# An embedding tower on one Trainium2 core: an eleventh table by matmul, a gather ring of 2 KB, and whole layer parts between the gram pieces

## The chip, the core and the metric

One core of a Trainium2 chip runs the whole kernel. The metric is the device time of one execution in microseconds. Three runs of the kernel before took 398.37, 398.69 and 398.92 us; the median is 398.69.

## What is computed

2048 samples have 128 dense features and one id in each of 26 tables with rows of 128 floats. One table has 125000 rows, eight have 12500, ten 1250 and seven 1000. The reference, cut to what matters:

```python
e = jnp.stack([tbl_0[ids[:, 0]], ..., tbl_25[ids[:, 25]]], axis=1)      # 2048 x 26 x 128
combined = jnp.concatenate([dense[:, None, :], e], axis=1)              # 2048 x 27 x 128
gram = jnp.einsum('bfd,bgd->bfg', combined, combined)                   # 27 x 27 a sample
z = jnp.concatenate([dense, gram[:, TRIU_I, TRIU_J]], axis=1)           # 128 + 351
h = jnp.concatenate([z, dense], axis=1)                                 # 607
h = jnp.maximum(h @ W_top1 + b_top1, 0.0)                               # 607 -> 512
h = jnp.maximum(h @ W_top2 + b_top2, 0.0)                               # 512 -> 256
y = h @ W_top3                                                          # 256 -> 1
```

Everything is float32.

## The kernel before, in words

The samples are cut into 16 tiles of 128, taken as 8 pairs (`i`): an even and an odd tile. Each engine has its own program, written out by hand, and they meet at semaphores. A table reaches the features in one of two ways.

**By gather** (16 tables, `GATHERED`). POOL issues one indirect DMA per tile and table (L328), 32 a pair, into `emb`, which has three tile slots. PE transposes four tables at a time into a PSUM bank (`flip`, L346) and ACT copies the bank into `feats` (`keep_flipped`, L544). A gather waits until the slot's old content is flipped, and for `pace` (L244): a place in PE's program, from the list of weighted steps in `places_of` (L212).

**By matmul** (the 10 smallest tables, `LOOKED_UP`; they stay in SBUF as an exact sum of two parts, `hi` and `lo`). A table is held in chunks of 125 rows: 8 chunks for 1000 rows, 10 for 1250. For each chunk DVE compares the ids of a pair's 256 samples with the row numbers and writes a matrix of zeros and ones (`mark`, L568, the operation at L580, "a mark"); PE multiplies `hi` and `lo` of the chunk by it (`look_up`, L350, L364). That is 7 x 8 + 3 x 10 = 86 marks and 172 matmuls a pair. `marks` is a ring of `MARK_CHUNKS` = 28 chunks. So DVE makes at most `AHEAD` = 7 halves of a table (28 marks) ahead of a pair's lookups. Two tables share a bank of the three in `flip_ps`, and ACT copies them out (`keep_looked`, L618, L622).

**The turn of a pair** on PE: all lookups of pair `i` (with `pair_rows` of the odd tile before among them), then `even_gram(i)` (L447), then `odd_gram(i)` (L474). The gram of a tile is 8 pieces (`gram`, L372, L386) of 16 float32 products of 27 x 27. Between the pieces stand the `flip`s of the next tile (4 a tile) and the layers of the pair before: `layer(i - 1, 0..3)` are the 512 outputs of the first layer, four products each; `layer(i - 1, 4)` and `5` the 256 of the second, four each; then `third_layer`. A part of a layer is split over several gaps with the argument `parts`. Of layer 3 the first two products stand before the even tile's last piece, the other two behind it. A float32 product of these layers and of the gram is recorded as two matmuls.

DVE, in order: `lay_out` (L549) of the even tile, which transposes the gram's result (L558) and copies the pairs out (L566), as soon as the even tile's last gram piece is done; 28 marks for the next pair; `lay_out` of the odd tile; the other 58 marks. For pairs 0 to 2 the flips of the even tile stand among the lookups instead of in the odd gram (`EARLY`).

**Start-up.** SP loads the ten tables into room that later holds something else (`places`, L124: five in `feats`, then `dots`, `w2_sb`, `hT`, `w1p_sb`; the tenth again in `dots`, when `lo` of the sixth is done, L291). ACT rounds each to `hi` (L674), DVE makes `lo` (L588) and the marks of pair 0. ACT's program has the lookups' copies among the roundings: the third copy and those of tile 0's flips stand behind the tenth rounding. The ids of the next pair (`id_cols`, 640 KB) are loaded when all marks of a pair are made (L302).

The four lines that say what waits in start-up:

```python
if s >= PLACES:
    sp.wait_ge(s_lo, place(s) + 1)          # SP, L291
act.wait_ge(s_raw[place(s)], ...)           # ACT, L673
dve.wait_ge(s_looked, g - MARKS_BACK[h] + 1)  # DVE, L578
```

## Time and profile before

| | |
|---|---|
| median of three runs | 398.69 us (398.37 to 398.92) |
| the profiled execution's own time | 400.2 us |
| its span in the profile | 398.3 us |
| PE busy / DVE / ACT / POOL | 364.5 / 261.1 / 137.0 / 247.2 us |
| marks (DVE L580) | 688, 211.5 us |
| lookup matmuls (PE L364) | 1376 |
| gathers (POOL L328) | 256, 247.0 us |
| mean granted TensorE clock | 0.983 of full speed |

The span is what the profile covers; the sums below are made against it. PE is the matmul engine (its weight loads are a row of their own, PEld), DVE the vector engine, ACT the scalar engine, POOL issues gathers and SP the plain DMAs. Matmul records overlap: what one costs is read from start to start. A busy share is an average over the start-up (to about 68 us), the seven turns and the tail (from about 372 us), which have different limits.

### The profile page before, as it was taken

The numbers are of one execution on the slowest core, as the hardware profiler recorded it, in microseconds if no ns is written. First come the engines' busy times: TensorE is split into PE (matmuls) and PEld (weight loads), VectorE is DVE, ScalarE is ACT, GpSimd is POOL, SyncE is SP. The second block draws the span as 40 slices with busy tenths as digits, with TensorE's granted clock in tenths as the row PEclk, the third lists the DMA queues.
The fourth block names the chain that finished last, engine by engine and source line by source line (L and its number), as shares of the span: only waits on it lengthen the run. The fifth ranks groups of instructions, "written<-read, shape, count | busy, mean of one in ns | idle before, by whom it ended". The sixth has DMA issues, their size and how long they took to land.

```text
span 398.3 us, 13947 instructions
## 1 busy us (share of the span) xinstructions
PE 364.5 (92%) x6192; PEld 309.7 (78%) x6192; DVE 261.1 (66%) x748; ACT 137.0 (34%) x195; POOL 247.2 (62%) x260
## 2 busy tenths in 40 slices
PE   0857758999999999999999999999999999999798
PEld 0757747987689977997789876997789877997575
DVE  2999864990699409990599519990699419980310
ACT  3545130343325234323433334323433334324222
POOL 6777777777677665776677666775677666720000
PEclk9998996999999999999999999999999999999989
DMA  7953442223112311323122311313121312200000
GB/s 242 411 195 110 149 144 57 54 55 120 49 42 55 113 43 44 82 53 115 43 55 55 114 49 44 81 54 109 48 51 53 116 47 51 54 22 2 5 2 0
DMA packets 13677, 31.72 MB, mean 80 GB/s; under 512 B 5301, under 2 KB 6205, under 8 KB 13618
## 3 DMA queue, kind: packets, MB, share of 16 engines
q0 software_dynamic: 8192, 16.79, 15.9%
q1 hardware_dynamic: 5426, 14.04, 9.7%
q8 instruction: 49, 0.80, 0.9%
q14 instruction: 10, 0.08, 0.1%
HBM read 30.81 MB, written 0.01 MB: 77 GB/s over the span
## 4 chain that ended last, share of the span: by engine, by line
PE 48%; DVE 44%; issue 4%; DMA 3%; ACT 1%; SPq 0%
DVE marks L580 37%; PE flip_ps L364 12%; PE mlp_ps L412 11%; PE gram_ps L386 9%; PE flip_ps L346 6%; PE mlp_ps L421 5%; PE mlp_ps L415 3%; DVE dots L558 3%; DVE lo L588 3%; DMA feats<-small_rows 1%; DMA id_cols<-ids_in_pairs 1%; DVE pair_dots L566 1%; PE mlp_ps L430 1%; PE pairs_ps L397 1%; ACT feats L622 0%
## 5 line engine op out<-in xcount | busy, mean ns | idle before, releaser
L328 POOL DMA_INDIRECT emb<-tbl,idx x256 | 247.0, 965 | 103.8 <-issue 55.8
L580 DVE TENSOR_SCALAR marks<-id_cols,row_no 125x256 fp32r<-125x256 int16 x688 | 211.5, 384 | 4.9 <-DMA id_cols<-ids_in_pairs 4.9
L364 PE MATMUL flip_ps<-marks,hi 125*128 125x256 f32 x688 | 172.2, 291 | 18.4 <-DVE marks L580 18.0
L364 PE MATMUL flip_ps<-marks,lo 125*128 125x256 f32 x688 | 167.9, 284 | 0.0
L364 PEld LDWEIGHTS flip_ps<-marks,hi 125*128 125x128 f32 x688 | 132.6, 193 | 26.0 <-issue 21.3
L364 PEld LDWEIGHTS flip_ps<-marks,lo 125*128 125x128 f32 x688 | 132.7, 193 | 0.0
L558 DVE STREAM_TRANSPOSE dots<-gram_ps 128x864 f32<-128x864 f32 (+1 forms) x32 | 25.2, 824 | 105.8 <-PE gram_ps L386 105.8
L622 ACT COPY feats<-flip_ps 128x512 f32<-128x512 f32 x40 | 46.7, 1167 | 124.4 <-PE flip_ps L364 119.4
L386 PEld LDWEIGHTS gram_ps<-feats 128*27 128x27 f32 x4096 | 43.0, 106 | 44.4 <-issue 43.3
L544 ACT COPY feats<-flip_ps 128x512 f32<-128x512 f32 x64 | 45.0, 725 | 64.9 <-PE flip_ps L346 62.8
L386 PE MATMUL gram_ps<-feats 128*27 128x27 f32 x4096 | 54.9, 192 | 10.2 <-issue 6.8
L412 PE MATMUL mlp_ps<-xT,w1p_sb 117*128 117x256 f32 x192 | 53.6, 391 | 0.5 <-ACT y_sb L657 0.5
L346 PE MATMUL flip_ps<-ident,emb 128*128 128x128 f32 x256 | 41.0, 285 | 2.7 <-ACT feats L622 2.3
L421 PE MATMUL mlp_ps<-hT,w_sb 128*128 128x256 f32 x128 | 36.6, 404 | 0.0
L412 PEld LDWEIGHTS mlp_ps<-xT,w1p_sb 117*128 117x128 f32 x192 | 32.5, 190 | 4.2 <-ACT xT L642 1.0
L649 ACT ACTIVATE hT<-mlp_ps,b_sb 128x256 f32<-128x256 f32 x48 | 22.7, 474 | 36.4 <-PE mlp_ps L415 23.2
L346 PEld LDWEIGHTS flip_ps<-ident,emb 128*128 128x128 f32 x256 | 27.0, 141 | 5.8 <-ACT feats L622 3.0
L421 PEld LDWEIGHTS mlp_ps<-hT,w_sb 128*128 128x128 f32 x128 | 23.0, 199 | 2.9 <-issue 0.3
L415 PE MATMUL mlp_ps<-dense_sb,w1d_sb 128*128 128x256 f32 x64 | 19.8, 391 | 0.0
L642 ACT COPY xT<-pairs_ps 117x384 f32<-117x384 f32 x16 | 8.4, 522 | 16.5 <-PE pairs_ps L397 16.5
L566 DVE COPY pair_dots<-dots 128x351 f32<-128x351 f32 x16 | 12.6, 788 | 0.5
L415 PEld LDWEIGHTS mlp_ps<-dense_sb,w1d_sb 128*128 128x128 f32 x64 | 11.1, 190 | 1.2
(23 smaller groups left out, 63.6 us busy)
## 6 DMA issues: line engine op xcount, KB each, us to landing
id_cols<-ids_in_pairs SPq DMA_DIRECT2D x7, 640.0 KB
emb<-tbl,idx POOLq DMA_INDIRECT x256, 2.5
feats<-small_rows SPq DMA_DIRECT2D x5, 512.0 KB, 7.5
dense_sb<-dense_columns SPq DMA_DIRECT2D x4, 256.0 KB, 9.2
w1p_sb<-w_pairs SPq DMA_DIRECT2D x1, 702.0 KB
hT<-small_rows SPq DMA_DIRECT2D x1, 640.0 KB, 12.6
w1p_sb<-small_rows SPq DMA_DIRECT2D x1, 640.0 KB, 14.5
dots<-small_rows SPq DMA_DIRECT2D x1, 640.0 KB, 4.0
```

The costliest lines, as they stand in the source:

```text
L328: nc.gpsimd.indirect_dma_start(emb[:, v, (f - 1) * P:f * P], None, tables[order[f - 1]][:, :], bass.IndirectOffsetOnAxis(ap=idx[:, t, orde ...
L346: last = nc.tensor.transpose(flip_ps[:, m % FLIP_BANKS, (f - 1) % GROUP, :], emb[:, v, (f - 1) * P:f * P], ident[:, :])
L364: last = nc.tensor.matmul(flip_ps[:, m % FLIP_BANKS, 2 * (s % 2):2 * (s % 2) + 2, :], part[s][0:R[s], half * x + c, :], marks[0:R[s], MARK ...
L386: last = nc.tensor.matmul(gram_ps[QUAD * j:QUAD * j + F, n, 0:F], row, row, start=True, stop=True)
L412: last = nc.tensor.matmul(bank, w1p_sb[0:CHUNK, c, q * P:(q + 1) * P], xT[0:CHUNK, c, :, :], start=(c == 0), stop=False)
L415: last = nc.tensor.matmul(bank, w1d_sb[:, q * P:(q + 1) * P], dense_sb[:, i % DENSE_PAIRS, :], start=False, stop=True)
L421: last = nc.tensor.matmul(bank, w2_sb[:, c, (q - H1C) * P:(q - H1C + 1) * P], h1T[:, c, :], start=(c == 0), stop=(c == H1C - 1))
L544: copy(feats[:, u, :, 1 + GROUP * k:1 + GROUP * k + n], flip_ps[:, m % FLIP_BANKS, 0:n, :].rearrange("d f p -> d p f")).then_inc(s_kept[u], 1)
L558: nc.vector.transpose(dots[:, g0 * QUAD:(g0 + n) * QUAD].rearrange("p (g f) -> p g f", f=QUAD), gram_ps[:, :, 0:n].rearrange("p n g -> p g ...
L580: last = nc.vector.tensor_scalar(marks[0:R[s], MARKS_AT[h] + c, :], id_cols[0:R[s], s, :], row_no[0:R[s], s, half * x + c:half * x + c + 1 ...
L622: nc.scalar.copy(feats[:, :, :, f:f + n].rearrange("d u p f -> d f u p"), flip_ps[:, m % FLIP_BANKS, 0:2 * n, :].rearrange("d (f u) p -> d ...
L649: nc.scalar.activation(h[:, c, :], mlp_ps[:, q % 2, 0:2 * P], ACT.Relu, bias=b[:, c:c + 1]).then_inc(s_act, 1)
```

## The change

Three things are changed. An eleventh table, of 1250 rows, is looked up by matmul, so 15 tables are gathered, in groups of 4, 4, 4 and 3. The room for it comes from the descriptor ring of the gathers, which had 16 KB a partition and now has 2 KB. And the layers stand in whole parts between gram pieces. The order in `places_of` and on ACT follows. The ring of marks stays at 28 chunks. Table eleven is loaded into `hT`, when `lo` of the eighth table is done (`place(10)` is 7).

```diff
-LOOKED_UP = 10
+LOOKED_UP = 11
...
-            places += [piece(even, 0)] + flips(odd, 0) + [piece(even, 1), piece(even, 2)] + flips(odd, 1)
-            places += part_of_layers(1) + [piece(even, 3), piece(even, 4)] + flips(odd, 2) + [piece(even, 5)]
-            places += part_of_layers(2) + [piece(even, 6)] + flips(odd, 3) + [piece(even, 7)] + part_of_layers(3)
...
+            for k in range(GROUPS):
+                places += [piece(even, 2 * k)] + flips(odd, k) + [piece(even, 2 * k + 1)] + part_of_layers(k + 1)
...
-                gram(2 * i, 0)
-                flip(2 * i + 1, 0)
-                layer(i - 1, 1, range(0, 1))
-                gram(2 * i, 1)
-                layer(i - 1, 1, range(1, 3))
-                gram(2 * i, 2)
...
-                layer(i - 1, 3, range(1, 2))
-                gram(2 * i, 7)
-                layer(i - 1, 3, range(2, 4))
+                for k in range(GROUPS):
+                    gram(2 * i, 2 * k)
+                    flip(2 * i + 1, k)
+                    gram(2 * i, 2 * k + 1)
+                    if k + 1 < H1C:
+                        layer(i - 1, k + 1)
...
-                layer(i - 1, 4, range(0, 2))
+                layer(i - 1, H1C)
                 gram(2 * i + 1, 0)
                 next_flip(0)
-                layer(i - 1, 4, range(2, 3))
                 gram(2 * i + 1, 1)
+                next_flip(1)
+                gram(2 * i + 1, 2)
                 pair_rows(2 * i)
-                layer(i - 1, 4, range(3, 4))
-                gram(2 * i + 1, 2)
-                next_flip(1)
-                layer(i - 1, 5, range(0, 1))
                 gram(2 * i + 1, 3)
-                layer(i - 1, 5, range(1, 3))
+                layer(i - 1, H1C + 1)
                 gram(2 * i + 1, 4)
                 next_flip(2)
-                layer(i - 1, 5, range(3, 4))
                 gram(2 * i + 1, 5)
-                third_layer(i - 1, range(0, 1))
+                next_flip(3)
                 gram(2 * i + 1, 6)
-                next_flip(3)
+                third_layer(i - 1)
                 gram(2 * i + 1, 7)
-                third_layer(i - 1, range(1, 2))
...
+            layer(last - 1, H1C)
             for part in range(PIECES):
                 gram(tiles - 1, part)
                 if part == 3:
                     pair_rows(tiles - 2)
-            layer(last - 1, 4)
-            layer(last - 1, 5)
+            layer(last - 1, H1C + 1)
             pair_rows(tiles - 1)
             third_layer(last - 1)
...
-    nc = bacc.Bacc("TRN2", target_bir_lowering=False, num_devices=1)
+    nc = bacc.Bacc("TRN2", target_bir_lowering=False, num_devices=1, dynamic_dma_scratch_size=2048)
```

PE, the end of the even tile's gram in a turn in the middle, before. A row is a run of like instructions; L412 and L415 are products of the first layer, L421 of the second, L386 a gram piece, L346 a flip:

```order
L346 MATMUL flip_ps<-ident,emb 128x128 x4
L412 MATMUL mlp_ps<-xT,w1p_sb 128x256
L386 MATMUL gram_ps<-feats 27x27 x16
L415 MATMUL mlp_ps<-dense_sb,w1d_sb 128x256
L412 MATMUL mlp_ps<-xT,w1p_sb 128x256
L386 MATMUL gram_ps<-feats 27x27 x16
L346 MATMUL flip_ps<-ident,emb 128x128 x4
L412 MATMUL mlp_ps<-xT,w1p_sb 128x256
L386 MATMUL gram_ps<-feats 27x27 x16
L412 MATMUL mlp_ps<-xT,w1p_sb 128x256
L415 MATMUL mlp_ps<-dense_sb,w1d_sb 128x256
L421 MATMUL mlp_ps<-hT,w_sb 128x256 x2
```

And of the change (its line numbers are one to two lower there):

```order
L345 MATMUL flip_ps<-ident,emb 128x128 x4
L385 MATMUL gram_ps<-feats 27x27 x16
L411 MATMUL mlp_ps<-xT,w1p_sb 128x256 x3
L413 MATMUL mlp_ps<-dense_sb,w1d_sb 128x256
L385 MATMUL gram_ps<-feats 27x27 x16
L345 MATMUL flip_ps<-ident,emb 128x128 x3
L385 MATMUL gram_ps<-feats 27x27 x16
L420 MATMUL mlp_ps<-hT,w_sb 128x256 x4
```

The last two products of layer 3 stood behind the even tile's last gram piece; now all four stand before its last two pieces, and behind the last piece comes layer 4 as a whole. The flip before the last piece has three tables in place of four.

ACT in start-up, before (L674 rounds a table, L622 copies a bank of lookups, L544 a flipped bank):

```order
L622 COPY feats<-flip_ps 128x2x256
L674 CAST hi<-dots 125x1280
L622 COPY feats<-flip_ps 128x2x256
L633 COPY feats<-dense_sb 128x256
L544 COPY feats<-flip_ps 128x128x4 x4
L622 COPY feats<-flip_ps 128x2x256 x2
```

And of the change:

```order
L599 COPY feats<-flip_ps 128x2x256
L651 CAST hi<-dots 125x1280
L651 CAST hi<-hT 125x1280
L599 COPY feats<-flip_ps 128x2x256
L610 COPY feats<-dense_sb 128x256
L521 COPY feats<-flip_ps 128x128x4 x3
L521 COPY feats<-flip_ps 128x128x3
L599 COPY feats<-flip_ps 128x2x256 x2
L599 COPY feats<-flip_ps 128x256
```

The eleventh rounding stands between the tenth and the third copy of lookups, and so ahead of the copies of tile 0's flips.

## Rows read from the trace of the kernel before

**Rows 1.** The page, chain that ended last: shares of the span by line

```profile
DVE marks L580 37%; PE flip_ps L364 12%; PE mlp_ps L412 11%; PE gram_ps L386 9%; PE flip_ps L346 6%; PE mlp_ps L421 5%; PE mlp_ps L415 3%; DVE dots L558 3%; DVE lo L588 3%; DMA feats<-small_rows 1%; DMA id_cols<-ids_in_pairs 1%; DVE pair_dots L566 1%; PE mlp_ps L430 1%; PE pairs_ps L397 1%; ACT feats L622 0%
```

**Rows 2.** Windows of one turn: length, then PE, PEld, DVE, ACT, POOL busy

```profile
225.67:237.22 11.55, 11.55 (x270) 8.33 (x268) 0.00 (x0) 4.87 (x8) 6.74 (x8) 1.00 0.30 101
237.22:248.73 11.51, 11.51 (x333) 8.29 (x332) 10.86 (x32) 4.88 (x9) 7.61 (x8) 1.00 0.18 48
248.73:270.17 21.44, 21.17 (x177) 20.90 (x177) 20.05 (x61) 6.06 (x8) 16.17 (x17) 1.00 0.27 71
```

**Rows 3.** Timeline of DVE, one turn: start, us, engine, line, operation, count

```profile
237.84 1.58 DVE L558 STREAM_TRANSPOSE dots<-gram_ps 128x864 f32<-128x864 f32 x2 [13.50 <-PE gram_ps L386]
...
240.16 8.45 DVE L580 TENSOR_SCALAR marks<-id_cols,row_no 125x256 fp32r<-125x256 int16 x28
248.53 1.56 DVE L558 STREAM_TRANSPOSE dots<-gram_ps 128x864 f32<-128x864 f32 x2
...
250.84 17.98 DVE L580 TENSOR_SCALAR marks<-id_cols,row_no 125x256 fp32r<-125x256 int16 x58
```

**Rows 4.** The chain in order of time: start us, us, what

```profile
268.87 1.46 PE flip_ps L364 x10
270.33 1.30 PE mlp_ps L412 x6
...
337.87 7.72 PE flip_ps L364 x64
```

**Rows 5.** Timeline of PE in the gram phase of the same turn

```profile
227.50 0.42 PE L386 MATMUL gram_ps<-feats 128*27 128x27 f32 x32
227.85 0.66 PE L346 MATMUL flip_ps<-ident,emb 128*128 128x128 f32 x4
228.34 0.60 PE L412 MATMUL mlp_ps<-xT,w1p_sb 117*128 117x256 f32 x2
228.87 0.42 PE L386 MATMUL gram_ps<-feats 128*27 128x27 f32 x32
229.22 1.13 PE L412 MATMUL mlp_ps<-xT,w1p_sb 117*128 117x256 f32 x4
230.28 0.42 PE L386 MATMUL gram_ps<-feats 128*27 128x27 f32 x32
```

**Rows 6.** Timeline of DVE in the last turn, where gathers end on the way

```profile
339.92 17.03 DVE L580 TENSOR_SCALAR marks<-id_cols,row_no 125x256 fp32r<-125x256 int16 x58
```

**Rows 7.** The gathers as a group (busy, mean ns, idle), and their landing

```profile
L328 POOL DMA_INDIRECT emb<-tbl,idx x256 | 247.0, 965 | 103.8 <-issue 55.8 <-PE gram_ps L386 20.5 <-PE flip_ps L364 12.9
...
emb<-tbl,idx POOLq DMA_INDIRECT x256, 2.5
```

**Rows 8.** Start-up, timelines of SP, then ACT, then DVE: start us, us

```profile
28.23 0.33 SPq L259 DMA_DIRECT2D dots<-small_rows  x1
...
32.22 1.26 ACT L674 CAST hi<-dots 125x1280 fp32r<-125x1280 f32 x1 [3.38 <-DMA dots<-small_rows]
...
34.43 1.53 DVE L588 TENSOR_TENSOR lo<-hT,hi 125x1280 fp32r<-125x1280 f32 x1
...
44.62 3.05 DVE L580 TENSOR_SCALAR marks<-id_cols,row_no 125x256 fp32r<-125x256 int16 x10
...
53.19 5.03 DVE L580 TENSOR_SCALAR marks<-id_cols,row_no 125x256 fp32r<-125x256 int16 x16 [4.93 <-DMA id_cols<-ids_in_pairs]
```

**Rows 9.** Start-up, timeline of PE: the first lookups after the flips

```profile
36.15 0.38 PE L364 MATMUL flip_ps<-marks,hi 125*128 125x256 f32 x1
...
38.81 0.41 PE L364 MATMUL flip_ps<-marks,lo 125*128 125x256 f32 x1
39.02 0.41 PE L364 MATMUL flip_ps<-marks,hi 125*128 125x256 f32 x1
```

**Rows 10.** The tail, timeline of PE, then DVE

```profile
377.37 5.41 PE L421 MATMUL mlp_ps<-hT,w_sb 128*128 128x256 f32 x16
...
379.13 0.77 DVE L566 COPY pair_dots<-dots 128x351 f32<-128x351 f32 x1
```

More of the change, by code:

```diff
@@ L82, in tower @@
     AHEAD = max(h for h in range(1, HALVES + 1) if sum(SIZES[:h]) <= MARK_CHUNKS)
-    assert CHUNKS == 3 and H1C == 4 and H2C == 2 and GROUPS == 4
+    assert H1C == GROUPS == 4 and H2C == 2 and PIECES == 2 * GROUPS
     ctx = ExitStack()
@@ L399, in pair_rows, with layer @@
                 last.then_inc(s_pairs, 1)
-            def layer(i, q, parts=range(4)):
+            def layer(i, q):
                 bank = mlp_ps[:, q % 2, 0:2 * P]
-                if q == 0 and 0 in parts:
+                if q == 0:
                     pe.wait_ge(s_xT, 2 * i + 2)
-                if q != 1 and (i or q) and 0 in parts:
+                if q != 1 and (i or q):
                     pe.wait_ge(s_act, STEPS * i + max(q - 1, 0))
-                for c in parts:
-                    if q < H1C and c < CHUNKS:
-                        last = nc.tensor.matmul(bank, w1p_sb[0:CHUNK, c, q * P:(q + 1) * P],
-                                                xT[0:CHUNK, c, :, :], start=(c == 0), stop=False)
-                    elif q < H1C:
-                        last = nc.tensor.matmul(bank, w1d_sb[:, q * P:(q + 1) * P],
-                                                dense_sb[:, i % DENSE_PAIRS, :], start=False, stop=True)
-                    else:
+                if q < H1C:
+                    for c in range(CHUNKS):
+                        nc.tensor.matmul(bank, w1p_sb[0:CHUNK, c, q * P:(q + 1) * P],
+                                         xT[0:CHUNK, c, :, :], start=(c == 0), stop=False)
+                    last = nc.tensor.matmul(bank, w1d_sb[:, q * P:(q + 1) * P],
+                                            dense_sb[:, i % DENSE_PAIRS, :], start=False, stop=True)
+                else:
+                    for c in range(H1C):
                         if q == H1C:
@@ L422, in layer, with third_layer @@
                                                 h1T[:, c, :], start=(c == 0), stop=(c == H1C - 1))
-                if 3 in parts:
-                    last.then_inc(s_mm, 1)
-            def third_layer(i, parts=range(H2C)):
-                for c in parts:
+                last.then_inc(s_mm, 1)
+            def third_layer(i):
+                for c in range(H2C):
                     pe.wait_ge(s_act, STEPS * i + H1C + c + 1)
@@ L431, in third_layer @@
                                             start=(c == 0), stop=(c == H2C - 1))
-                if H2C - 1 in parts:
-                    last.then_inc(s_mm, 1)
+                last.then_inc(s_mm, 1)
             def looking_up(i, groups=range(LOOK_GROUPS)):
@@ L451, in even_gram @@
                 layer(i - 1, 0)
-                gram(2 * i, 0)
-                flip(2 * i + 1, 0)
-                layer(i - 1, 1, range(0, 1))
-                gram(2 * i, 1)
-                layer(i - 1, 1, range(1, 3))
-                gram(2 * i, 2)
-                flip(2 * i + 1, 1)
-                layer(i - 1, 1, range(3, 4))
-                gram(2 * i, 3)
-                layer(i - 1, 2, range(0, 2))
-                gram(2 * i, 4)
-                flip(2 * i + 1, 2)
-                layer(i - 1, 2, range(2, 3))
-                gram(2 * i, 5)
-                layer(i - 1, 2, range(3, 4))
-                layer(i - 1, 3, range(0, 1))
-                gram(2 * i, 6)
-                flip(2 * i + 1, 3)
-                layer(i - 1, 3, range(1, 2))
-                gram(2 * i, 7)
-                layer(i - 1, 3, range(2, 4))
+                for k in range(GROUPS):
[4 more added lines that the diff above has]
+                        layer(i - 1, k + 1)
             def odd_gram(i):
```

28 lines of the change are left out of this document (11 added, 17 removed).

## The prediction

> **What bounds the kernel now.** I read the page's chain first. Its largest line is DVE's marks, 37% of the span, ahead of every line of PE [rows 1], although PE is busy 364.5 us and DVE 261.1. A kernel bound by PE all the time would not show that, so I cut one turn of the middle into three windows at PE's milestones [rows 2]: the even tile's gram with layers 0 to 3 (11.55 us, DVE idle all of it), the odd tile's gram (11.51 us, DVE busy 10.86), the lookups (21.44 us, DVE busy 20.05). The turn is 44.5 us. DVE's timeline shows why [rows 3]: it waits 13.50 us for the even tile's last gram piece, starts at 237.84, and from there has no pause to speak of. `lay_out`, 28 marks (8.45 us), the second `lay_out`, 58 marks (17.98 us) end at 268.82. PE then does the last half table and layer 0 starts at 270.33 [rows 4]. The loop that sets the turn is thus: DVE from even gram to last mark, 31.0 us; PE's last half table, 1.5; PE's even half of the gram up to DVE's next start, 12.0. The sum is 44.5. The odd half of the gram is not in it: it runs under DVE's first `lay_out` and 28 marks, and ends just as these do.
>
> What PE alone would need is close behind. At full clock 64 lookup matmuls take 7.72 us, 0.12 each [rows 4], so 86 chunks take 20.7 us and with `pair_rows` 21.1; the window has 21.44. PE has 0.3 us a turn to spare, no more.
>
> POOL is not on the path. A gather is 0.965 us [rows 7] and one starts every 1.25 us at the closest; 32 take 40.0 us of the turn's 44.5. Among the waits there is none of PE for a gather, while POOL waits 20.5 us for gram pieces alone, to keep its pace [rows 7].
>
> **The price of a mark.** Two stretches of 58 marks differ: 17.98 us with 14 gathers beside them [rows 3], 17.03 us in the last turn with 9, where the gathers end [rows 6]. The difference of 0.95 us over 5 gathers is 0.19 us a gather, which leaves (17.98 - 14 x 0.19)/58 = 0.264 us a mark. The eleventh table removes gathers and adds marks, and a window of 68 marks will hold about 14 gathers still, since POOL's pace follows PE: 68 x 0.264 + 14 x 0.19 = 20.6 us, 2.6 more than now. The bounds are 2.6 and, at 0.31 us a mark throughout, 3.1.
> The Trainium skill (SBUF — State Buffer, Who interferes with whom) says that a vector instruction with one SBUF input, outside the two-port modes, does not contend with GpSimd at all. If the marks are such, the gathers are not why the two stretches differ, a mark is 0.31 us whatever POOL does, and the sum below would be 3.5 us higher. The rows look otherwise, and I go by them.
>
> **The change, part by part.**
> - *Ten more marks a pair.* They come after `AHEAD` = 28, in the stretch that is on the loop: +2.6 us in each of turns 1 and 3 to 6. In the last turn PE, not DVE, ended the lookups, by 0.3 us, so +2.3 there. In turn 2 PE is slower than DVE (its flips of tile 4 stand among the lookups): PE has 20 matmuls more, 20 x 0.12 = 2.4 us, and its odd half is 0.9 us shorter (a point below), which leaves +1.4; DVE's own path comes out the same there.
> - *Twenty more matmuls a pair*, 2.4 us, beside the marks: hidden, since DVE is slower per chunk. If DVE's marks cost nothing more, they would be what is late next.
> - *Layer 3 whole in the even half.* Two float32 products move from behind the even tile's last piece to ahead of it. A product is two recorded matmuls, six of which take 1.30 us [rows 4]: 0.43 us each. The even half is on the loop, so +0.87 us a turn. The flip of three tables in place of four gives back 0.10. Net +0.77 us, seven times.
> - *Whole parts.* Do they save by fewer switches? Behind a gram piece two products take 1.06 us where 0.87 is their work; one product between a flip and a gram piece takes 0.53 us, where 0.43 is work [rows 5]. So going from and to gram pieces costs 0.10 us each. But the change leaves something between every two gram pieces, seven gaps in the even half before and after. No switch goes. I cost the regrouping at nothing, with bounds of -0.3 and +0.3 us a turn.
> - *The odd half* loses 0.87 + 0.10, gets back some 0.3 since `third_layer` is no longer spread, and ends near 10.8 us after the last even piece, where DVE's `lay_out` may start only when its 28 marks are made, at 11.3. It is hidden, with PE's slack now about 1.3 us a turn. If the odd half were stretched by more than that, it would count.
> - *DVE's transposes before the odd gram*: they end 2.2 us after the last even piece starts. Before, 2.0 us of layer work stood there; now layer 4 (4 x 0.43 + 0.20 = 1.93 us), and the odd gram starts at 2.28. Cover still just holds.
> - *Two gathers a pair fewer*, 16 x 1.25 us of POOL: nothing, as no one waits for POOL. Through a ring of 2 KB they cost what they do now, I take: a gather lands in 2.5 us [rows 7] and starts every 1.25, so two or three are under way at once. The trace shows no full ring; the price is bounded below by 0 and above by a gather that waits for the one before it, 0.965 + 2.5 us.
> - *Start-up.* Table eleven goes to `hT`, whose load may begin when DVE's eighth `lo` is done, at 35.9. The tenth was issued at 28.23 and was ready for ACT at 32.22, 4.0 us [rows 8]; so the eleventh is at 39.9. ACT's third copy of lookups and tile 0's flips stand behind that rounding, and PE's fourth group of lookups behind them. That group began 3.9 us after the last rounding did (36.15 against 32.22, [rows 8, 9]), so now at 43.8. PE is idle meanwhile, and restarts at the lower clock: 0.213 us a matmul (38.81 to 39.02, [rows 9]). The seventh table's 16 matmuls end at 47.3. DVE has by then filled the ring of 28 chunks and stands before the tenth table's marks, which it began at 44.62 [rows 8]. From 47.3: five marks and the wait for the next half (to about 50.4), `lo` 1.4, ten marks 3.0, to 54.8. Before, the last mark ended at 47.6. The start-up is 7.3 us longer (4.4 of it would be the table's own marks and `lo`, the rest is the wait). The ids of pair 1 are loaded after that and all follows: DVE waited 4.93 us for them [rows 8], and will again. Bounds: 6.0 with PE at full clock, 8.3 with a longer slow stretch.
> - *The tail.* Layer 4 of pair 6 moves from behind the last gram to ahead of it, where PE waited for DVE's transposes. Behind the gram, layers 4 and 5 took 5.41 us together [rows 10], at less than full clock; one of them leaves, 2.7 us; `pair_rows` can't start before DVE's copy is through at 379.90 [rows 10], against 382.6 now, so at most 2.7 is gained. I take -2.4; bounds -2.7 and 0.
>
> Sum: start-up 7.3; turn 1 2.6 + 0.4 (there POOL runs unpaced, so two more gathers fall beside the marks) + 0.8 = 3.8; turn 2 1.4 + 0.8 = 2.2; turns 3 to 6 4 x 3.4 = 13.6; turn 7 2.3 + 0.8 = 3.1; tail -2.4. Together **+27.6 us**. The span of 398.3 becomes 425.9, the profiled execution's 400.2 becomes 427.8, and the median 398.69 becomes 426.3.
>
> **The rivals.**
> - *PE becomes the bound.* If the marks come cheaper than I think (fewer gathers beside them), PE alone has: even half 12.3, odd half 10.8, lookups 192 x 0.12 + 0.4 = 23.5, together 46.6 us, 2.1 over now. Then turns 3 to 6 give 8.4 and turn 7 2.6: 7.3 + 3.8 + 2.2 + 8.4 + 2.6 - 2.4 = 21.9, so 420.6 us. For it: PE's slack is only 1.3 us a turn. Against it: ten marks would have to cost under 1.3 us, and the lowest price in the rows is 0.264 each.
> - *The ring is too small.* If a gather must wait for room until an earlier one has landed, up to 3.5 us each, POOL becomes the bound from 47.8/30 = 1.6 us a gather. At 1.9 us, 240 gathers take 456 us, and with the 47 us that follow the last gather now the kernel takes some 503 us. Against it: two or three gathers in flight are few. Nothing in the trace shows a ring's limit.
> - *Faster, because the gathers were the bound.* If POOL's train of 256 x 1.25 us = 320 us set the time and the rest hung on it, 16 gathers fewer would give -20 us: 378.7 us. It would decide if PE stood waiting for gathers. Against it: POOL is the one that waits, by its pace [rows 7], and PE and DVE have no time for the extra work.
>
> **The numbers.** My forecast has 0.76, PE as the bound 0.16, the ring 0.05, the faster case 0.01; 0.02 is left for an effect much smaller than any of these (half each to no change and to faster). The range takes in PE as the bound, with a start-up 1.3 cheaper and 0.3 us a turn gained by the whole parts (417), and upward the marks at 0.31 us (+3.5), no gain in the tail (+2.4) and a start-up 1 us longer: 433. The ring's case is left out. A measurement can tell 0.2% (0.8 us) from no change. Faster by more than that has 0.02, within it 0.01, slower 0.97.
>
> **What would show it.** Right: turns of about 47.9 us in the middle; DVE's stretch of 68 marks near 20.6 us, directly before the last half table of each turn; DVE's idle time before the even `lay_out` about 14.3 us; PE stalls of 1 to 2 us in the lookups for marks; ACT's eleventh rounding near 40, PE idle from 32 to 42, the last mark of pair 0 near 55. Wrong: turns of 46 us with PE never waiting; gathers longer than 1 us or PE waiting for them; an even half of the gram shorter than 12 us (then whole parts do save something); stalls in the odd half that reach DVE's second `lay_out`.

## The result, and the profile after

| | kernel before | the change |
|---|---|---|
| median of 4 runs each | 398.81 us (398.37 to 399.10) | 426.87 us (426.37 to 428.43) |
| ratio, 95% interval | | 1.0711 (1.0681 to 1.0741) |
| profiled execution: time, span | 400.2, 398.3 us | 426.6, 424.8 us |
| mean granted clock of TensorE | 0.983 | 0.976 |
| PE busy, DVE busy | 364.5, 261.1 us | 381.5, 278.6 us |

The change is 7% slower. The forecast was 426.3 us with a range of 417 to 433, slower with 0.97. The median is met within 0.6 us (the span, 424.8 against 425.9, within 1.1), but that is partly luck: the start-up was off by 3.5 us and the turns together by 3.8, in opposite directions. A table shows it best. Each stretch ends at the start of a `lay_out` on DVE, of tile 1 or of the next even tile, and its length is compared before and after.

| stretch | forecast | measured (spans) |
|---|---|---|
| start-up, up to tile 1's `lay_out` | +7.3 | +10.8 (65.67 to 76.45) |
| turn 1 | +3.8 | +2.7 |
| turn 2 | +2.2 | +2.3 |
| turns 3 to 6 | 4 x 3.4 | 2.8, 2.8, 2.7, 2.9 |
| turn 7 | +3.1 | +2.7 |
| tail, behind the last even `lay_out` | -2.4 | -3.15 (27.65 to 24.50) |
| sum | +27.6 | +26.5 |

One plain word on the experiments: three of their four series fell on chips, called slow below, on which the kernel before had a median of 500 to 505 us (the series with `order_alone_b` and `grouped` had it at 398.43 us), so of these only distances inside a trace and ratios are used, and each ratio is of the fast runs alone while the medians are of all runs.

**The chain.** The page of the change, shares of the span by engine and line, to be held against [rows 1]:

```profile
PE 64%; DVE 27%; issue 4%; DMA 2%; ACT 1%; SPq 0%
PE flip_ps L363 24%; DVE marks L557 23%; PE mlp_ps L411 11%; PE gram_ps L385 10%; PE flip_ps L345 8%; PE mlp_ps L420 6%; PE mlp_ps L413 3%; DVE lo L565 2%; DMA feats<-small_rows 1%; DVE dots L535 1%; PE mlp_ps L428 1%; PE pairs_ps L396 1%; DMA hT<-small_rows 1%; DVE pair_dots L543 1%; ACT hi L651 1%
```

The marks had 37% before and have 23% now, though there are more of them; PE's lookups had 12% and have 24%. The shares overstate the move. In turns 2, 3, 4 and 6 the chain leaves DVE 11 marks before the last one and follows PE's last 30 lookup matmuls, and in turns 5 and 7 it stays on PE through all lookups; but in each of turns 4, 5 and 7 the last mark ends 1.32 us before the lookups do, which is PE's last half table. DVE and PE end each of these turns almost together.

**One turn.** Windows of a turn in the middle, cut as [rows 2] are: length, then PE, PEld, DVE, ACT, POOL busy:

```profile
199.01:211.30 12.29, 12.29 (x274) 9.43 (x272) 0.00 (x0) 4.66 (x8) 7.60 (x9) 1.00 0.31 102
211.30:222.00 10.70, 10.70 (x328) 8.17 (x328) 9.88 (x32) 4.89 (x9) 7.58 (x4) 1.00 0.12 28
222.00:246.38 24.38, 24.02 (x196) 23.18 (x196) 23.02 (x71) 6.79 (x8) 17.97 (x18) 1.00 0.21 51
```

The even half grew from 11.55 to 12.29 us, the odd half shrank from 11.51 to 10.70, the lookups grew from 21.44 to 24.38. The cut at 222.00 lies 0.21 us behind PE's first lookup, at 221.79; cut there, as [rows 2] is, the odd half is 10.50 us and the lookups are 24.59. The turn is 47.4 us, forecast 47.9. PE is busy 47.0 of it.

DVE's timeline over the same turn answers to [rows 3]; the last two rows are of the next turn:

```profile
211.82 1.58 DVE L535 STREAM_TRANSPOSE dots<-gram_ps 128x864 f32<-128x864 f32 x2 [14.13 <-PE gram_ps L385]
...
214.12 7.57 DVE L557 TENSOR_SCALAR marks<-id_cols,row_no 125x256 fp32r<-125x256 int16 x28
221.96 1.58 DVE L535 STREAM_TRANSPOSE dots<-gram_ps 128x864 f32<-128x864 f32 x2 [0.27 <-PE gram_ps L385]
...
224.29 20.77 DVE L557 TENSOR_SCALAR marks<-id_cols,row_no 125x256 fp32r<-125x256 int16 x68
...
261.49 7.91 DVE L557 TENSOR_SCALAR marks<-id_cols,row_no 125x256 fp32r<-125x256 int16 x28
...
272.16 20.11 DVE L557 TENSOR_SCALAR marks<-id_cols,row_no 125x256 fp32r<-125x256 int16 x68
```

Three numbers are as forecast: 68 marks in 20.77 us (20.6), DVE idle 14.13 us ahead of the even `lay_out` (14.3), and the even half above (12.3). Two are not. The 28 marks ahead take 7.57 us where [rows 3] had 8.45, and DVE then waits 0.27 us for the odd gram. So the first part of the loop is no longer DVE's `lay_out` and 28 marks but PE's odd half: from one `lay_out` to the other it is 10.14 us (211.82 to 221.96), where [rows 3] has 10.69. In the next turn, turn 5, the 28 take 7.91 and the 68 take 20.11. With the same cuts, the odd half, the lookups and the even half are

| turn | odd half | lookups | even half | together | the 68 marks |
|---|---|---|---|---|---|
| 4 | 10.50 | 24.59 | 12.29 | 47.4 | 20.77 |
| 5 | 10.99 | 23.93 | 12.29 | 47.2 | 20.11 |
| 7 | 10.49 | 23.70 | 12.30 | 46.5 | 19.86 |

The lookups are as long as the marks make them. Turn 5's odd half holds a stall of PE (0.26 us of idle time before 264.24, with nothing to wait for) that the others have not.

**A gather that hangs.** The cheaper 28 marks have a visible companion. POOL's timeline around the same stretch of an earlier turn (DVE makes its 28 marks from 166.74 to 174.31 there):

```profile
167.48 0.94 POOL L327 DMA_INDIRECT emb<-tbl,idx  x1 [0.74 <-PE flip_ps L345]
169.70 4.73 POOL L327 DMA_INDIRECT emb<-tbl,idx  x1 [1.27 <-PE gram_ps L385]
```

One gather lasts 4.73 us and ends at 174.43, 0.12 us after the marks. It happens so in four of the turns, 4.73 to 4.76 us each. In turn 1 it is worse: 80 marks run from 78.75 to 100.79, and one gather hangs for most of that, to 94.73. It doesn't last to the end of the marks, but there is a break in them where it ends: DVE does nothing from 94.60 to 94.70, the only such break among the 80.

```profile
79.59 15.14 POOL L327 DMA_INDIRECT emb<-tbl,idx  x1 [1.96 <-PE flip_ps L363]
```

The group's mean went from 965 ns [rows 7] to

```profile
L327 POOL DMA_INDIRECT emb<-tbl,idx x240 | 265.5, 1106 | 113.0 <-issue 47.9
```

Nobody waits for such a gather. While it hangs, POOL issues no others, and the marks beside it run at their price alone: 28 x 0.264 = 7.4 us.

**Start-up.** DVE in the change, to be held against [rows 8]:

```profile
44.16 1.48 DVE L565 TENSOR_TENSOR lo<-dots,hi 125x1280 fp32r<-125x1280 f32 x1
48.80 3.00 DVE L557 TENSOR_SCALAR marks<-id_cols,row_no 125x256 fp32r<-125x256 int16 x10 [3.16 <-PE flip_ps L363]
51.72 1.48 DVE L565 TENSOR_TENSOR lo<-hT,hi 125x1280 fp32r<-125x1280 f32 x1
53.12 3.04 DVE L557 TENSOR_SCALAR marks<-id_cols,row_no 125x256 fp32r<-125x256 int16 x10
...
61.64 5.03 DVE L557 TENSOR_SCALAR marks<-id_cols,row_no 125x256 fp32r<-125x256 int16 x16 [4.88 <-DMA id_cols<-ids_in_pairs]
67.21 1.58 DVE L535 STREAM_TRANSPOSE dots<-gram_ps 128x864 f32<-128x864 f32 x2 [0.54 <-PE gram_ps L385]
...
76.45 1.58 DVE L535 STREAM_TRANSPOSE dots<-gram_ps 128x864 f32<-128x864 f32 x2 [6.82 <-PE gram_ps L385]
```

and what it waited for, the eleventh table's load on SP, its rounding on ACT, and PE's restart:

```profile
36.94 0.33 SPq L258 DMA_DIRECT2D hT<-small_rows  x1
```

```profile
41.06 1.26 ACT L651 CAST hi<-hT 125x1280 fp32r<-125x1280 f32 x1 [6.56 <-DMA hT<-small_rows]
42.22 1.09 ACT L599 COPY feats<-flip_ps 128x512 f32<-128x512 f32 x1
```

```profile
43.37 1.93 PE L345 MATMUL flip_ps<-ident,emb 128*128 128x128 f32 x7 [9.55 <-ACT feats L599]
44.98 0.58 PE L363 MATMUL flip_ps<-marks,hi 125*128 125x256 f32 x1
45.35 0.42 PE L363 MATMUL flip_ps<-marks,lo 125*128 125x256 f32 x1
```

The load takes 4.1 us as forecast (36.94 to 41.06), PE stands 9.55 us and restarts at 0.21 us a matmul; the granted clock is 0.50 from 43.37 to 48.50, the lower of its two levels (1.2 against 2.4 GHz). The last mark of pair 0 ends at 56.1, 8.5 us later than before; 54.8 was forecast. What the forecast did not have comes behind it. PE's gram of tiles 0 and 1:

```profile
61.09 0.41 PE L385 MATMUL gram_ps<-feats 128*27 128x27 f32 x31
63.22 0.42 PE L385 MATMUL gram_ps<-feats 128*27 128x27 f32 x33 [1.72 <-issue]
...
68.94 1.34 PE L385 MATMUL gram_ps<-feats 128*27 128x27 f32 x118 [1.79 <-DVE dots L535]
72.33 2.06 PE L385 MATMUL gram_ps<-feats 128*27 128x27 f32 x128 [2.05 <-issue]
76.06 0.34 PE L385 MATMUL gram_ps<-feats 128*27 128x27 f32 x10 [1.67 <-issue]
```

"Issue" is time in which PE waited for nothing that the profile shows. Tile 1's gram has two such stalls, 2.05 and 1.67 us; before it had one of 1.81. Tile 0's has stalls of 1.72 (shown) and 1.22 us, and 0.76 ahead of it; before there were 1.41 within it and 1.22 ahead of it, and DVE did not wait for them. Together they turn +8.45 at DVE's 16 marks (61.64 against 53.19) into +9.1 at tile 0's `lay_out` and +10.8 at tile 1's.

**The tail.** PE, the answer to [rows 10]:

```profile
403.82 0.29 PE L385 MATMUL gram_ps<-feats 128*27 128x27 f32 x10
405.33 1.23 PE L385 MATMUL gram_ps<-feats 128*27 128x27 f32 x118 [1.22 <-issue]
406.49 1.99 PE L420 MATMUL mlp_ps<-hT,w_sb 128*128 128x256 f32 x8
409.06 0.59 PE L396 MATMUL pairs_ps<-ident,pair_dots 128*117 128x128 f32 x3 [0.57 <-DVE pair_dots L543]
```

One layer (8 matmuls, 1.99 us, at full clock) and a wait of 0.57 stand where 5.41 us of two layers stood: 2.57 us to `pair_rows` in place of 5.24. The other half microsecond is the smaller stall, 1.22.

### The profile page after: what moved, and what is told of

It reads as the page before. It is cut to its first block, busy times and chain, and to the rows that moved or that the text cites. A ratio compares the mean times of both kernels' runs of the same rounds, so it can differ in the third digit from the quotient of the medians.

```text
span 424.8 us, 14318 instructions
## 1 busy us (share of the span) xinstructions
PE 381.5 (90%) x6336; PEld 332.0 (78%) x6336; DVE 278.6 (66%) x829; ACT 141.9 (33%) x204; POOL 265.7 (63%) x244
## 4 chain that ended last, share of the span: by engine, by line
PE 64%; DVE 27%; issue 4%; DMA 2%; ACT 1%; SPq 0%
PE flip_ps L363 24%; DVE marks L557 23%; PE mlp_ps L411 11%; PE gram_ps L385 10%; PE flip_ps L345 8%; PE mlp_ps L420 6%; PE mlp_ps L413 3%; DVE lo L565 2%; DMA feats<-small_rows 1%; DVE dots L535 1%; PE mlp_ps L428 1%; PE pairs_ps L396 1%; DMA hT<-small_rows 1%; DVE pair_dots L543 1%; ACT hi L651 1%
## 5 line engine op out<-in xcount | busy, mean ns | idle before, releaser
L327 POOL DMA_INDIRECT emb<-tbl,idx x240 | 265.5, 1106 | 113.0 <-issue 47.9
L557 DVE TENSOR_SCALAR marks<-id_cols,row_no 125x256 fp32r<-125x256 int16 x768 | 227.1, 372 | 8.1 <-DMA id_cols<-ids_in_pairs 4.9
L363 PE MATMUL flip_ps<-marks,hi 125*128 125x256 f32 x768 | 191.9, 292 | 19.1 <-DVE marks L557 18.4
L363 PE MATMUL flip_ps<-marks,lo 125*128 125x256 f32 x768 | 185.8, 284 | 0.0
L363 PEld LDWEIGHTS flip_ps<-marks,hi 125*128 125x128 f32 x768 | 148.4, 193 | 26.3 <-issue 19.1
L363 PEld LDWEIGHTS flip_ps<-marks,lo 125*128 125x128 f32 x768 | 148.5, 193 | 0.0
L599 ACT COPY feats<-flip_ps 128x512 f32<-128x512 f32 (+1 forms) x48 | 52.1, 1086 | 137.9 <-PE flip_ps L363 132.4
L411 PE MATMUL mlp_ps<-xT,w1p_sb 117*128 117x256 f32 x192 | 49.0, 391 | 0.5 <-ACT y_sb L634 0.5
L521 ACT COPY feats<-flip_ps 128x512 f32<-128x512 f32 x64 | 41.0, 662 | 22.9 <-PE flip_ps L345 21.9
L626 ACT ACTIVATE hT<-mlp_ps,b_sb 128x256 f32<-128x256 f32 x48 | 22.7, 474 | 76.7 <-PE mlp_ps L413 46.6
L420 PE MATMUL mlp_ps<-hT,w_sb 128*128 128x256 f32 x128 | 31.5, 391 | 0.0
```

Of the source, the lines that this page charges most:

```text
L327: nc.gpsimd.indirect_dma_start(emb[:, v, (f - 1) * P:f * P], None, tables[order[f - 1]][:, :], bass.IndirectOffsetOnAxis(ap=idx[:, t, orde ...
L363: last = nc.tensor.matmul(flip_ps[:, m % FLIP_BANKS, 2 * (s % 2):2 * (s % 2) + 2, :], part[s][0:R[s], half * x + c, :], marks[0:R[s], MARK ...
L411: nc.tensor.matmul(bank, w1p_sb[0:CHUNK, c, q * P:(q + 1) * P], xT[0:CHUNK, c, :, :], start=(c == 0), stop=False)
L420: last = nc.tensor.matmul(bank, w2_sb[:, c, (q - H1C) * P:(q - H1C + 1) * P], h1T[:, c, :], start=(c == 0), stop=(c == H1C - 1))
L521: copy(feats[:, u, :, 1 + GROUP * k:1 + GROUP * k + n], flip_ps[:, m % FLIP_BANKS, 0:n, :].rearrange("d f p -> d p f")).then_inc(s_kept[u], 1)
L557: last = nc.vector.tensor_scalar(marks[0:R[s], MARKS_AT[h] + c, :], id_cols[0:R[s], s, :], row_no[0:R[s], s, half * x + c:half * x + c + 1 ...
```

## The experiments

### The order alone, and on a usual chip

```diff
-LOOKED_UP = 11
+LOOKED_UP = 10
...
-    nc = bacc.Bacc("TRN2", target_bir_lowering=False, num_devices=1, dynamic_dma_scratch_size=2048)
+    nc = bacc.Bacc("TRN2", target_bir_lowering=False, num_devices=1)
```

(against the change: its order, ten tables, the old ring)

> The new order (whole layer parts, layer 4 ahead of the last gram) with ten tables by matmul and the ring of 16 KB. My theory: two float32 products of layer 3 come into the even half of the gram, +0.87 us in each of seven turns (the flip stays at four tables), and the tail gives back 2.4 to 3.1: +3 to +4 us, about 402. DVE's idle time before the even lay_out grows from 13.5 to 14.4. Rival: whole parts save switches, so that the even half is not longer: 396 to 397, the tail's gain alone.

> The new order with ten tables by matmul and the ring of 16 KB, once more, since all runs of the first series, those of the kernel before too, stood 100 us above their usual time. My theory: layer 3's last two products in the even half cost 0.87 us in each of seven turns, and layer 4 ahead of the last gram gives back 2.4 to 3.1 us in the tail: +3 to +4 us against the kernel before, 402 to 403; DVE's idle time before the even lay_out 14.4 us. Rival: whole parts save switches and the even half is no longer: 396, the tail's gain alone.

`order_alone` gave 497.21 us where the kernel before took 504.45, which tells nothing about one part. `order_alone_b`: 401.99 us (400.90 to 403.19, 12 runs) against 398.43, ratio 1.0087 (1.0064 to 1.0110), so +3.5 us, as expected. Its DVE, one turn:

```profile
240.76 1.58 DVE L535 STREAM_TRANSPOSE dots<-gram_ps 128x864 f32<-128x864 f32 x2 [14.33 <-PE gram_ps L385]
...
243.08 8.52 DVE L557 TENSOR_SCALAR marks<-id_cols,row_no 125x256 fp32r<-125x256 int16 x28
251.52 1.56 DVE L535 STREAM_TRANSPOSE dots<-gram_ps 128x864 f32<-128x864 f32 x2
...
253.84 17.77 DVE L557 TENSOR_SCALAR marks<-id_cols,row_no 125x256 fp32r<-125x256 int16 x58
...
285.93 1.58 DVE L535 STREAM_TRANSPOSE dots<-gram_ps 128x864 f32<-128x864 f32 x2 [14.32 <-PE gram_ps L385]
```

The idle time ahead of the even `lay_out` is 14.33 us where it was 13.50: +0.83, and 0.87 was forecast for layer 3's two products (the flip keeps four tables here). A turn is 45.2 us, +0.7. The tail is 25.1 us, -2.6. The marks cost nearly what they did (8.52 and 17.77 against 8.45 and 17.98), and in this stretch no gather hangs. So the reordering by itself loses: whole layers bring back nothing in the middle, and layer 3 within the even half is on the loop.

### The table alone

```diff
-LOOKED_UP = 10
+LOOKED_UP = 11
...
-    nc = bacc.Bacc("TRN2", target_bir_lowering=False, num_devices=1)
+    nc = bacc.Bacc("TRN2", target_bir_lowering=False, num_devices=1, dynamic_dma_scratch_size=2048)
```

(against the kernel before; eleven tables need the small ring)

> The kernel before with the eleventh table by matmul and the ring of 2 KB, in the old order. If marks and order add up: the change less 0.87 us in seven turns, plus the tail's 2.4 to 3.1: 423 to 425. Theory P (PE is the bound of the changed turn by now): a turn is what PE needs, 46.6 us, so layer 3 moved out gives 0.7 at most and the time is 424 to 426. Turns near 46.5 us by both; PE's waits for marks tell them apart: none to speak of by P, over 0.5 us a turn by my forecast.

> The kernel before with the eleventh table and the ring of 2 KB, in the old order, once more on an undisturbed chip. The new order alone cost 3.5 us. If marks and order add up, the table costs the rest: 426.9 - 3.5 = 423.4 us. Theory P (with eleven tables PE alone needs 46.6 us a turn, so the order is partly hidden or the table partly): 424 to 426. The turn by either is 46.4 to 46.8 us.

Both fell on slow chips: 496.23 against 504.45 us (0.9883, 0.9800 to 0.9966), and 493.39 against 500.01 (0.9945, 0.9902 to 0.9988). What the table costs on a usual chip is thus not measured alone; the change's 28.1 us less the order's 3.5 leaves 24.6, by subtraction only. The turns of 46.4 to 46.8 us that were expected can't be read from these chips either. A point worth keeping: on both of them the same eleventh table comes out slightly ahead.

### The ring

```diff
-    nc = bacc.Bacc("TRN2", target_bir_lowering=False, num_devices=1)
+    nc = bacc.Bacc("TRN2", target_bir_lowering=False, num_devices=1, dynamic_dma_scratch_size=2048)
```

(`ring_alone`, `ring_alone_b` and `ring_alone_c`, against the kernel before; `ring_8k` is the change with 8192 in place of 2048)

> The kernel before with the descriptor ring of the gathers cut from 16 KB to 2 KB a partition, nothing else. Theory R (the ring fills): about every 15th gather takes 2 us or more, as in the changed kernel (there 4.7 and 2.0 us twice a turn); while it hangs no descriptors are written beside the marks, so the 28 marks made ahead take about 7.6 us in place of 8.45. PE has only 0.3 us a turn to spare, so the time falls by 0 to 2 us (397 to 399). Rival N (the long gathers come from the longer stretch of marks or the new order): no gather over 3 us, the 28 marks stay at 8.4, the time stays at 398.7.

> The kernel before with the descriptor ring cut from 16 KB to 2 KB, once more. Theory R (a full ring makes every 15th gather wait): gathers over 4 us twice a turn. Theory L (a gather that meets a stretch of marks at an unlucky moment is locked out until the stretch pauses; in the changed kernel the one of 4.73 us begins at 169.70 and ends at 174.43, where 28 marks end at 174.31, and with 8 KB on the disturbed chip gathers of 4.8 us were there too): no gather over 3 us, but for one or two, and the time within 0.3% of the kernel before.

> The kernel before with the descriptor ring cut from 16 KB to 2 KB, once more. Theory R (a full ring makes a gather wait): gathers of 4 us or more twice a turn, as in the changed kernel. Theory L (locked out by a stretch of marks, whatever the ring): at most one or two gathers over 2.5 us, as with 16 KB, the 28 marks at 8.4 us, and the time within 0.3% of the kernel before.

> The changed kernel with a ring of 8 KB in place of 2 KB (it fits). Theory R: the long gathers are gone but for one in about 60, the 28 marks ahead take 8.4 us again in place of 7.6, and turns come to the 47.9 us of my prediction in place of 47.3: some 3 us slower than the change, about 430. Rival N: the gathers of 4.7 us stay, turns and time as in the change, 426.9.

The small ring alone: 505.41 against 504.45, 507.77 against 500.01, and 503.25 against 505.21 us, the last with a ratio of 0.9984 (0.9935 to 1.0032). All are from slow chips, and the last interval reaches 0.65% down and 0.3% up. The change with four times the ring: 505.23 against 504.45 (0.9918, 0.9818 to 1.0018), and its hanging gathers are the same:

```profile
253.64 4.77 POOL L327 DMA_INDIRECT emb<-tbl,idx  x1 [1.94 <-PE gram_ps L385]
```

```profile
250.01 7.58 DVE L557 TENSOR_SCALAR marks<-id_cols,row_no 125x256 fp32r<-125x256 int16 x28
```

253.64 + 4.77 = 258.41, and the marks end at 257.59, 0.8 us earlier and not 0.12. The theory that I had formed on seeing the change's trace, that a ring of 2 KB fills and a gather waits for room, falls between 2 and 8 KB: with 8 KB the gather hangs for the same 4.8 us, once a turn, beside the same 28 marks.

The small ring alone did not come out as either expectation had it. In `ring_alone_c` a gather hangs in every turn, 5.27 to 5.31 us in five of them, and the 28 marks take 7.4 to 7.6 us and not 8.4; `ring_alone` has three gathers over 4 us and `ring_alone_b` four. But with 16 KB, on a slow chip as well, `order_alone` has four over 4 us, up to

```profile
325.09 14.59 POOL L327 DMA_INDIRECT emb<-tbl,idx  x1 [0.76 <-PE flip_ps L363]
```

So a small ring is not needed for a hang. On usual chips the three traces with 16 KB (`before`, `order_alone_b`, `grouped`) have at most one gather over 2.5 us, 3.55 at most, and the only trace with 2 KB is that of the change; whether ring or table makes the hang regular there, and whether the total time is the same with either ring, was not measured.

### Gathers taken away

```diff
-            for t in range(tiles):
+            for t in range(SLOTS):
...
-                pe.wait_ge(s_emb[v][k], 16 * len(features_in(k)) * (t // SLOTS + 1))
+                pe.wait_ge(s_emb[v][k], 16 * len(features_in(k)))
```

> The kernel before with gathers for the first three tiles only; later tiles use what these left in the slots, so 13 of 16 tiles have the wrong gathered features. It leaves the marks alone on DVE from about 60 us on. My price (0.264 us a mark and 0.19 for each gather beside them): the 58 marks take 15.3 us in place of 17.98, the 28 take 7.4 in place of 8.45, PE becomes the bound of the turn with 44.2 us and the time is 396 to 397. Rival (gathers do not touch the marks): 58 marks in 18.0 us, turn and time as before.

This is the kernel before, with gathers for the first 3 tiles only; 13 of the 16 tiles take the gathered rows of an earlier one. It settles the price of a mark. DVE in the middle:

```profile
253.77 1.58 DVE L558 STREAM_TRANSPOSE dots<-gram_ps 128x864 f32<-128x864 f32 x2 [15.43 <-PE gram_ps L386]
...
256.05 7.44 DVE L580 TENSOR_SCALAR marks<-id_cols,row_no 125x256 fp32r<-125x256 int16 x28
264.45 1.58 DVE L558 STREAM_TRANSPOSE dots<-gram_ps 128x864 f32<-128x864 f32 x2 [0.96 <-PE gram_ps L386]
...
266.80 15.32 DVE L580 TENSOR_SCALAR marks<-id_cols,row_no 125x256 fp32r<-125x256 int16 x58
```

58 marks take 15.32 us, 0.264 each, where they take 17.98 beside 14 gathers: 0.19 us a gather. These are the two numbers that the forecast drew from two rows. The turn is 43.8 us, 0.7 less than before, though DVE's path is 3.7 us shorter (2.66 and 1.0): PE is the bound at once, and DVE waits for the odd gram too. PE's slack was 0.7 us and not the 0.3 of the forecast: its 172 lookup matmuls with `pair_rows` take 20.78 us when no mark is late (264.69 to 285.47), where 21.1 was worked out and [rows 2] has 21.44.

The rule weighed ahead of the forecast (the Trainium skill, SBUF — State Buffer, Who interferes with whom) says of instructions with at most one SBUF input and outside the two-port modes that they don't contend with GpSimd. The marks are slower beside gathers (17.98 against 15.32 us), so it doesn't free them. The same section says that a transfer that seems held up by a vector instruction is one whose descriptors GpSimd writes; the hanging gathers, which POOL issues, agree.

The whole kernel took 412.14 us, with a ratio of 0.8465 (0.8418 to 0.8511) to the kernel before, by runs of it at 486.62 and 486.99; the 396 to 397 us that were expected can't be tested there.

### Gram pieces in twos, layer 3 out of the even half

```diff
-            places += [piece(even, 0)] + flips(odd, 0) + [piece(even, 1), piece(even, 2)] + flips(odd, 1)
...
+            places += two(even, 0) + flips(odd, 0) + flips(odd, 1) + part_of_layers(1)
+            places += two(even, 1) + flips(odd, 2) + part_of_layers(2) + two(even, 2) + flips(odd, 3)
+            places += two(even, 3) + part_of_layers(3) + part_of_layers(4)
+            places += two(odd, 0) + flips(following, 0) + flips(following, 1) + two(odd, 1) + part_of_layers(5)
+            places += two(odd, 2) + flips(following, 2) + flips(following, 3) + part_of_layers(6)
+            return places + two(odd, 3)
```

(against the kernel before, ten tables; PE, ACT and the tail follow, with layer 4 ahead of the last gram as in the change)

> The kernel before (ten tables, ring of 16 KB) in an order of my own: gram pieces in twos without anything between, layer 3 whole behind the last even piece, layer 4 ahead of the last gram in the tail. If a switch from and to gram pieces costs 0.10 us each way, eight of the sixteen gaps of a turn fall away, 1.6 us of PE; the even half loses 0.8 of it and 0.87 of layer 3, and the loop of DVE's marks goes from 44.5 to about 43.1 us a turn. With the tail: 398.7 - 7 x 1.4 - 2.5 = 386 to 388 us. Rival: PE runs out of instructions in denser gram (it waited 1.8 us for no signal after some 130 matmuls in a row in start-up and tail): stalls of 1 to 2 us a turn appear as issue waits, and the time is 396 to 400.

Measured 396.24 us (395.31 to 397.75, 12 runs), ratio 0.9943 (0.9920 to 0.9966). It beats both kernels, but by 2 us where 10 were expected. Its DVE and a part of its PE:

```profile
280.01 1.58 DVE L543 STREAM_TRANSPOSE dots<-gram_ps 128x864 f32<-128x864 f32 x2 [12.48 <-PE gram_ps L388]
...
291.83 1.58 DVE L543 STREAM_TRANSPOSE dots<-gram_ps 128x864 f32<-128x864 f32 x2 [1.05 <-PE gram_ps L388]
...
324.49 1.58 DVE L543 STREAM_TRANSPOSE dots<-gram_ps 128x864 f32<-128x864 f32 x2 [12.49 <-PE gram_ps L388]
```

```profile
270.69 1.20 PE L388 MATMUL gram_ps<-feats 128*27 128x27 f32 x64
271.82 1.09 PE L348 MATMUL flip_ps<-ident,emb 128*128 128x128 f32 x8
```

The idle time ahead of the even `lay_out` fell by 1.0 us, to 12.48, of which 0.87 is layer 3. But the odd half, which took the layer over, now ends 1.05 us after DVE's 28 marks, and DVE waits there: the four turns in the middle stay at 44.5 to 44.8 us. Turns 1, 2 and 7 and the tail have room for it and are 1.2, 1.1, 1.0 and 1.1 us shorter. Fewer switches bring little, since two pieces in a row (64 matmuls, 0.70 us by twice a piece's 0.35) do not always take 0.7: the four pairs of this even half take 1.13 (270.69 to 271.82), 0.82, 0.67 and 0.67. The stalls of 1 to 2 us that the rival had expected are not there.

### ACT's eleventh rounding moved back

```diff
+                if s == PLACES + 1:
+                    keep_looked(0, 2)
+                    keep_dense(0)
+                    keep_all(0)
...
-            keep_looked(0, 2)
-            keep_dense(0)
...
-                if i < EARLY:
+                if 0 < i < EARLY:
```

(against the change)

> The changed kernel with one edit: ACT rounds the eleventh table after the third copy of lookups, the dense copy and the four copies of tile 0's flips, not ahead of them. My theory of the start-up (PE's fourth group of lookups waits for this rounding, and DVE's ring of marks for PE): PE resumes near 37 in place of 45, DVE does not stand still before the tenth table's marks (3.2 us in the change), the last mark of pair 0 is at 53 in place of 56.1, and the whole is 3.0 to 4.5 us faster than the change: 422.5 to 424. Rival: the start-up is bound by DVE's work and the loads, and PE's pause is hidden: under 1 us.

> The changed kernel with ACT's eleventh rounding behind the third copy of lookups, the dense copy and tile 0's flips, once more, since the last series stood 100 us above its usual times throughout. My theory: PE's fourth group of lookups no longer waits for table eleven; PE resumes near 37, DVE has no pause before the tenth table's marks, the last mark of pair 0 is near 53 in place of 56.1, and the whole is 3.0 to 4.5 us faster than the change: a ratio of 1.060 to 1.064 to the kernel before where the change has 1.071. Rival: PE's pause is hidden by DVE's work and the loads: under 1 us, a ratio of 1.069 or more.

509.67 us against 500.01, and 527.46 against 505.21, both on slow chips, on which the change itself was not timed; of the total nothing can be said. The trace shows the stretch. DVE in `start_fix_b`:

```profile
47.89 1.48 DVE L565 TENSOR_TENSOR lo<-w1p_sb,hi 125x1280 fp32r<-125x1280 f32 x1
...
53.66 3.05 DVE L557 TENSOR_SCALAR marks<-id_cols,row_no 125x256 fp32r<-125x256 int16 x10
56.62 1.49 DVE L565 TENSOR_TENSOR lo<-hT,hi 125x1280 fp32r<-125x1280 f32 x1
58.02 3.04 DVE L557 TENSOR_SCALAR marks<-id_cols,row_no 125x256 fp32r<-125x256 int16 x10
```

From `lo` of the ninth table to the last mark of pair 0 it is 13.1 us, against 16.3 in the change (39.79 to 56.08), and the pause of 3.16 us ahead of the tenth table's marks is gone. 3.1 us were expected. The slow chip is not what removed it: `ring_8k`, which has the rounding where the change has it, ran on such a chip too and keeps a pause of 2.36 us there (ahead of 57.64), with 15.3 us for the stretch (49.63 to 64.93). So that rounding's place is what cost the start-up its pause; whether the total time keeps the gain stays open.

## Why the prediction was right, and where it was not

- *DVE's marks as the bound.* Right for the larger part of the loop: +2.6 us for ten marks (20.77 for 68; the lone price and the price of a gather beside it came out to the digit without gathers), +0.87 for layer 3 (+0.83 with the order alone), even half 12.3 (12.29). The net +0.77 ahead of the even `lay_out` was +0.63 (14.13 against 13.50), and the odd half of 10.8 was 10.50. One sign did not come: PE's stalls of 1 to 2 us for marks. In turn 4 it waits for them 0.21 us that the profile records, since lookups and marks run nearly side by side.
- *"Turns 3 to 6, 4 x 3.4"* was too high by 0.5 to 0.7 a turn. The step that failed is a silent one: that the 28 marks ahead keep their 8.45 us. They took 7.57 in the turns in which a gather hung beside them, and 7.91 in turn 5, where none hung but POOL's pace put only four beside them. Not all of the 0.9 us was kept, since PE was then late with the odd gram by 0.27. The forecast gave the odd half PE's slack of a whole turn, 1.3 us, before it would count; against DVE's 28 marks it had 0.5 by its own numbers (10.8 against 11.3), and with cheaper marks none. What sets the hang off is not shown. With 8 KB it is the same as with 2, and neither a small ring nor the eleventh table is needed for it: `ring_alone_c` has ten tables and `order_alone` has ten tables and 16 KB.
- *PE as the bound* was given 46.6 us a turn. Turn 7, whose chain is PE's alone, took 46.5, and there too the lookups end 1.32 us after the last mark. PE by itself would need less, by my estimate some 46.0: 20.78 us for the lookups without late marks plus 20 x 0.12 for the added ones, 10.5 and 12.3 for the halves. Turns 3, 4 and 6 are 47.4 us since their 68 marks take 20.8, and turn 5 is 47.2 with 20.1 for the marks and 0.5 for the stall. So the rival was half true: PE's odd half replaced DVE's 28 marks in the loop, but the 68 marks stayed in it.
- *"Turn 1, 3.8"* came out 2.7. The two more gathers that I put beside its marks did not run there: one gather hung through 15.14 us of them, and 80 marks took 22.04 us where 70 had taken 21.76. From 77.32 to the even half the chain is PE's lookups and flips, with one copy of ACT's between.
- *"Start-up 7.3"* was 3.5 too low, the largest miss of a single term, and 2.5 past its upper bound of 8.3. Load, rounding, restart and slow clock went as worked out. The last mark of pair 0 was 8.5 later, not 7.3; 0.8 of this is a first table that came later in this execution (`lo` at 9.14 against 8.37). The other 2.3 are PE's stalls in the grams of tiles 0 and 1, which I had taken as unchanged. The ids' wait was as forecast, 4.88.
- *The tail, -2.4*, was -3.15, past the bound of -2.7. The bound took PE's stall in the last gram as fixed at 1.82; it was 1.22.
- *Regrouping at nothing, the ring at nothing.* The first is confirmed by the order alone: +0.7 a turn, no more than layer 3's products cost. For the second the trace shows no wait of anybody on a gather; times of the ring alone on a usual chip are missing. Gathers longer than 1 us were named as a sign of being wrong: they came, and only made the marks beside them cheaper.
- *Faster, and the ring too small at 503 us*: neither came. Nobody waits for POOL in the change.

The errors of +3.5 in the start-up, -3.8 in the turns and -0.75 in the tail nearly cancel, and the time is right by that. The range of 417 to 433 would have held either of the two larger ones alone.

## What to carry to other kernels

Find the loop of waits that sets a turn, and ask of each moved instruction whether it lies in the part that is on the loop: here two layer products cost 0.83 us a turn on one side of a milestone and nothing on the other, until the other side's slack is used up (`grouped` moved layer 3 to the odd half, and DVE then waited 1.05 us there). That slack is to be taken against the milestone that the side has to meet, not against the whole turn. A loop gives back at most its lead over the next bound, however much is taken off it (DVE's path 3.7 us shorter, turn 0.7). And a start-up of 60 us should be costed instruction by instruction like a turn, its unexplained stalls included.

## What the runs showed of the chip that I had not expected

- A gather beside an unbroken train of vector instructions may hang until the train has a break: 4.73 us under 28 marks, to 0.12 us past their end, and 15.14 us under 80, to 0.13 us past the start of a break of 0.10 us; most others beside the same kind of marks pass in 0.94. With 8 KB the hang ended 0.8 us behind the marks, so the end of the marks is not all of it.
- PE stands for 1.2 to 2.1 us with nothing to wait for, after some 100 to 170 gram matmuls in a row: at 72.33, 76.06 and 405.33 in the change, and before in both the start-up and the tail (1.81, 1.82). Two gram pieces back to back take up to 1.13 us in place of 0.70. What stands beside these stalls is a packet of 16 KB on the queue of instructions (q8): all six stalls within a gram in the change, and all four in the kernel before, end 1.2 to 1.6 us after such a packet has ended. The one before 72.33 follows a packet from 69.91 to 70.97. So PE most likely waits there for its own instructions; no run tests it by changing them.
- On the slow chips the chain of the small ring alone (`ring_alone_c`) reads

```profile
PE 52%; another core or an unknown queue 21%; issue 13%; DVE 12%; DMA 1%; ACT 1%; SPq 0%
```

  and that of the kernel with few gathers, on a chip just as slow,

```profile
PE 88%; issue 9%; ACT 1%; DVE 1%
```

  Some 75 us, between the 486.62 and 486.99 of the kernel before and 412.14, thus went with the gathers, and with them the chain's waits on an unknown queue. The Trainium skill (Runtime: NRT & Kernel Launch, Instruction fetch mechanics) says that an engine's sequencer fetches its instructions by DMA through a queue of its own. That gathers delay these fetches on such a chip would fit both rows; it was not tested by itself.
